# Four windowed-attention blocks on one core: constants loaded in two pieces, the first group's statistics gathered per image, bias tables on GpSimd, last stores in smaller parts

## The reference, cut to what matters

```
def _layernorm_hwc(x, scale, bias):                    # first block
    mean = jnp.mean(x, axis=(1, 2, 3), keepdims=True)
    var = jnp.var(x, axis=(1, 2, 3), keepdims=True)
    return (x - mean) * jax.lax.rsqrt(var + EPS) * scale + bias

attn = einsum('bhnd,bhmd->bhnm', q, k) + bias + mask    # blocks 2 to 4: one bias table, masks fixed by the window
x = x + softmax(attn) @ v @ proj_w + proj_b
m = gelu(_ln(x) @ fc1_w + fc1_b)                        # last block
x = x + _ln(m) @ fc2_w + fc2_b
```

## Time and profile before

| What | us |
|---|---|
| median of 3 runs | 7809.69 |
| lowest and highest of them | 7807.17, 7815.15 |
| the profiled execution's own time | 7816.85 |
| its span, first to last instruction | 7815.1 |

### The profile page before, as it was taken

One profiled execution on the slowest core, in us unless ns is written; L12 is line 12 of the kernel. 1 busy time (PEld: TensorE's weight loads), 2 busy tenths in 40 slices (PEclk: granted clock), 3 DMA queues, 4 the chain that ended last, 5 costly groups with the idle time before them and its releaser, 6 DMA issues.

```text
span 7815.1 us, 310674 instructions
## 1 busy us (share of the span) xinstructions
PE 7327.9 (94%) x109686; PEld 5700.3 (73%) x109686; DVE 6100.8 (78%) x18297; ACT 4899.6 (63%) x8745; POOL 5299.8 (68%) x6555
## 2 busy tenths in 40 slices
PE   5999999999899999999989999999999999999998
PEld 3777777777677777777767777777776777777777
DVE  6878878777786887877878687786787778778677
ACT  3746647557674765746767475574677647567467
POOL 4956657567795765757789476674778857567576
PEclk9999999999999999999999999999999999999999
DMA  2101101010110110101011011010101101011010
GB/s 62 39 11 30 52 12 33 11 36 17 25 40 30 35 47 17 33 7 43 10 31 51 19 34 43 22 33 7 45 4 37 57 11 33 14 27 30 11 42 25
DMA packets 309909, 227.60 MB, mean 29 GB/s; under 512 B 217379, under 2 KB 305766, under 8 KB 306344
## 3 DMA queue, kind: packets, MB, share of 16 engines
q1 hardware_dynamic: 307858, 215.98, 10.3%
q10 hardware_dynamic: 1622, 6.13, 0.2%
HBM read 117.62 MB, written 104.37 MB: 28 GB/s over the span
## 4 chain that ended last, share of the span: by engine, by line
POOL 35%; issue 27%; PE 22%; DVE 7%; POOLq 4%; DVEq 2%; ACT 1%; ACTq 0%
POOL S L654 17%; PE ps L1082 8%; PE ps L1055 7%; POOL G L644 7%; POOL xn L670 4%; POOL rstd L626 4%; DVE xn L1257 2%; DVE bst L1108 2%; PE ps L1069 2%; DVE x L1419 1%; PE ps L901 1%; DVEq L1257 1%; POOL mv L697 1%; PE ps L932 1%; POOLq L476 1%
## 5 line engine op out<-in xcount | busy, mean ns | idle before, releaser
L654 POOL TENSOR_TENSOR S<-S,mx 113x588 f32<-113x588 f32 (+1 forms) x2048 | 2059.0, 1009 | 896.3 <-DVE mx L1299 878.2
L777 ACT ACTIVATE S<-S 113x588 f32<-113x588 f32 (+1 forms) x2048 | 1246.9, 609 | 823.9 <-POOL S L654 809.2
L959 PE MATMUL ps<-turn,S 113*123 113x113 f32 (+2 forms) x8704 | 1329.2, 278 | 103.7 <-ACT PT L782 73.7
L1299 DVE TENSOR_REDUCE mx<-S 113x12 f32<-113x588 f32 (+1 forms) x2048 | 1359.4, 664 | 70.6
L782 ACT ACTIVATE PT<-ps 123x490 f32<-123x490 f32 (+1 forms) x2048 | 1051.1, 513 | 458.7 <-PE ps L959 438.6
L959 PEld LDWEIGHTS ps<-turn,S 113*123 113x123 f32 (+2 forms) x8704 | 927.7, 167 | 514.9 <-ACT PT L782 328.9
L1055 PEld LDWEIGHTS ps<-w,G 128*98 128x98 f32 x12288 | 1150.5, 167 | 159.3 <-issue 87.6
L1055 PE MATMUL ps<-w,G 128*98 128x96 f32 (+1 forms) x12288 | 1151.3, 250 | 0.0
L1082 PE MATMUL ps<-h,w 97*128 97x392 f32 x3072 | 1124.1, 502 | 9.1 <-ACT G L865 9.1
L1296 DVE TENSOR_TENSOR S<-ps,bias 113x588 f32<-113x588 f32 (+1 forms) x1536 | 963.9, 628 | 181.9 <-PE ps L948 135.2
L932 PEld LDWEIGHTS ps<-Va,PT 123*49 123x49 f32 (+1 forms) x18432 | 755.8, 125 | 326.3 <-ACT PT L782 255.0
(11 more groups left out here) (94 smaller groups left out, 12145.3 us busy)
## 6 DMA issues: line engine op xcount, KB each, us to landing
v_between<-Vd SPq DMA_DIRECT2D x384, 165.4 KB
Va<-v_between SPq DMA_DIRECT2D x768, 41.3 KB
Vb<-v_between SPq DMA_DIRECT2D x768, 27.6 KB
v_between<-Vd SPq DMA_DIRECT2D x128, 153.1 KB
Vl<-v_between SPq DMA_DIRECT2D x256, 76.6 KB
out_dram<-x SPq DMA_DIRECT2D x15, 1176.0 KB
x<-x_dram SPq DMA_DIRECT2D x14, 1176.0 KB
mask<-mask_dram SPq DMA_DIRECT2D x258, 37.5 KB
```

The source lines that it names most:

```text
L654: pool.tensor_tensor(v, v, m, ALU.subtract).then_inc(a_sub, 1)
L777: act.activation(S[:, p, 0:nh * N], S[:, p, 0:nh * N], ACT.Exp).then_inc(a_exp, 1)
L959: last = pe.transpose(ps[0:rows, PT_BANK, PAIR * b:PAIR * b + TOK], S[:, p, at:at + rows], turn[:, :])
L1299: dve.reduce_max(mx[:, s, 0:nh], S[:, s, 0:n].rearrange("p (h k) -> p h k", k=N), axis=AX.X).then_inc(a_mx, 1)
```

## The change

Four things are done. `load` splits a constant of 97 or 113 rows into its first 96 or 112 rows and its last row, two transfers. The 12 bias tables are made on POOL, ahead of its `fill`, as soon as the raw bias and `mask4` have landed, both counted on `s_braw`. The first group's statistics are taken as 32 `bn_stats` and one `bn_aggr` over all of them per image, which gives mean and variance of the image's pairs per partition at once; `norm` works on 4 columns in place of 128, has two `busy` matmuls fewer ahead of its second average, and takes up the correction of `w3` and `c2` while POOL raises to -0.5, so that PE waits for it only behind `norm`. At the end image 2 is stored when 24 quads are done, the first half of image 3 when 28 are, and its second half, in two parts from SP and ACT, behind `s_fin`.

```diff
+        def last_pairs(eng, a, b):
+            eng.dma_start(out[GROUPS - 1, :, a * C:b * C],
+                          x[:, (GROUPS - 1) % 2 * NP + a:(GROUPS - 1) % 2 * NP + b, :].rearrange("p a c -> p (a c)")
+                          ).then_inc(s_out, 16)
...
         def load(eng, dst, src):
-            eng.dma_start(dst, src).then_inc(s_const, 16)
-            n_const[0] += 16
+            rows = dst.shape[0]
+            cuts = (0, rows - 1, rows) if rows in (C + 1, TOK) else (0, rows)
+            for a, b in zip(cuts, cuts[1:]):
+                eng.dma_start(dst[a:b, :], src[a:b, :]).then_inc(s_const, 16)
+                n_const[0] += 16
...
             tokens(sp, GROUPS - 1, True, s_out, 0, IMGS // 2)
+            sp.wait_ge(m_res, GROUPS * LAYER_QUADS - NQ // 4)
+            tokens(sp, GROUPS - 1, True, s_out, IMGS // 2, IMGS - 1)
+            sp.wait_ge(m_res, GROUPS * LAYER_QUADS - NQ // 8)
+            last_pairs(sp, NP - 2 * 4 * QUAD, NP - 4 * QUAD)
             sp.wait_ge(s_fin, GROUPS)
-            tokens(sp, GROUPS - 1, True, s_out, IMGS // 2, IMGS, turn=0, turns=2)
+            last_pairs(sp, NP - 4 * QUAD, NP - 2 * QUAD)
...
             pool.wait_ge(s_memset, 2)
+            pool.wait_ge(s_braw, 32)
+            for l in range(1, LAYERS):
+                nh = HEADS[l]
+                for v in range(4):
+                    last = pool.tensor_tensor(bias[l][:, v, :].rearrange("p (h k) -> p h k", k=N),
+                                              stage(l).rearrange("p (h k) -> p h k", k=N),
+                                              mask4[:, v, :].unsqueeze(1).to_broadcast([P, nh, N]), ALU.add)
+            last.then_inc(s_tab, 1)
+            pool.wait_ge(s_tab, 1)
...
             act.wait_ge(s_fin, GROUPS)
-            tokens(act, GROUPS - 1, True, s_out, IMGS // 2, IMGS, turn=1, turns=2)
+            last_pairs(act, NP - 2 * QUAD, NP)
...
-            pe.wait_ge(s_w3, 2)
...
                     for n in range(2):
-                        busy(2, 4)
+                        busy(2, 4 if n == 0 else 2)
                         average_of(0, 0, 2, n)
+                    pe.wait_ge(s_w3, 2)
...
-            quad_steps(dve, 0, load_stats, 2, 0, NQ // 2)
-            dve.wait_ge(s_x, 16 * HALF_DMAS)
-            quad_steps(dve, 0, load_stats, 2, NQ // 2, NQ)
+            for image in range(IMGS):
+                if image == IMGS // 2:
+                    dve.wait_ge(s_x, 16 * HALF_DMAS)
+                for a in range(PAIRS_IMG):
+                    last = dve.bn_stats(bfirst[:, image, a, :], x[:, image * PAIRS_IMG + a, :])
+                last.then_inc(s_first, 1)
+                dve.wait_ge(s_first, image + 1)
+                dve.bn_aggr(ifirst[:, image, :], bfirst[:, image, :, :].rearrange("p a s -> p (a s)")).then_inc(s_gather, 1)
...
-            dve.wait_ge(s_w3ps, 1)
-            dve.tensor_tensor(w3[:, :, 0:C], w3[:, :, 0:C], ps[:, 0, 0:C].unsqueeze(1).to_broadcast([P, HC, C]),
-                              ALU.subtract)
-            dve.tensor_tensor(c2[:, LAYERS - 1, :], c2[:, LAYERS - 1, :], ps[:, 1, 0:C], ALU.add).then_inc(s_w3, 1)
...
...
                 def norm():
-                    image_sums(0, 0, 2)
-                    image_squares(0, 0, 2)
-                    image_var(0, 0, 2)
-                    image_scale(0, 0, 2)
+                    dve.tensor_scalar(isum[:, :], mean, float(PAIRS_IMG), None, ALU.mult).then_inc(s_avg, 1)
+                    dve.wait_ge(s_avg, 2)
+                    dve.tensor_copy(imean[:, :], ps[0:PAIR, O_BANK, 0:IMGS]).then_inc(s_chain, 1)
+                    dve.tensor_tensor(mean, mean, imean[:, :], ALU.subtract).then_inc(s_chain, 1)
+                    dve.tensor_tensor(mean, mean, mean, ALU.mult).then_inc(s_chain, 1)
+                    dve.tensor_tensor(mean, mean, var, ALU.add).then_inc(s_chain, 1)
+                    dve.tensor_scalar(isum[:, :], mean, float(PAIRS_IMG), None, ALU.mult).then_inc(s_avg, 1)
+                    dve.tensor_scalar(ivar[:, :], ps[0:PAIR, O_BANK, 0:IMGS], EPS, None, ALU.add).then_inc(s_nm, 1)
+                    dve.wait_ge(s_w3ps, 1)
+                    dve.tensor_tensor(w3[:, :, 0:C], w3[:, :, 0:C],
+                                      ps[:, 0, 0:C].unsqueeze(1).to_broadcast([P, HC, C]), ALU.subtract)
...
+                    dve.wait_ge(s_pow, 1)
+                    dve.tensor_copy(scales, irstd[:, :].unsqueeze(2).to_broadcast(every)).then_inc(s_chain, 1)
+                    dve.scalar_tensor_tensor(mean, imean[:, :], -1.0, irstd[:, :], ALU.mult,
+                                             ALU.mult).then_inc(s_chain, 1)
+                    dve.tensor_copy(shifts, mean.unsqueeze(2).to_broadcast(every)).then_inc(s_nmr, 1)
+                    dve.wait_ge(s_tab, 1)
```

More of the change, by code:

```diff
@@ L195, in build @@
         irstd = sb("irstd", [PAIR, IMGS])
+        ifirst = sb("ifirst", [PAIR, IMGS, 2])
         ident = sb("ident", [P, P])
@@ L240, in build @@
         shift3 = room[:, SHIFTS:SHIFTS + HC * P].rearrange("p (c q) -> p c q", c=HC)
+        bfirst = room[0:PAIR, SHIFTS + (HC + 1) * P:SHIFTS + (HC + 1) * P + 6 * NP].rearrange(
+            "p (i a s) -> p i a s", i=IMGS, s=6)
         share3 = room[:, SHIFTS + HC * P:SHIFTS + (HC + 1) * P]
@@ L289, in build @@
         s_w3 = sem("ln3_weights_scaled")
+        s_first = sem("first_image_stats")
+        s_gather = sem("first_image_gathered")
         s_w3ps = sem("ln3_weight_sums_done")
@@ L582, in _ @@
             tokens(sp, GROUPS - 1, True, s_out, 0, IMGS // 2)
+            sp.wait_ge(m_res, GROUPS * LAYER_QUADS - NQ // 4)
+            stand(sp)
+            tokens(sp, GROUPS - 1, True, s_out, IMGS // 2, IMGS - 1)
+            sp.wait_ge(m_res, GROUPS * LAYER_QUADS - NQ // 8)
+            stand(sp)
+            last_pairs(sp, NP - 2 * 4 * QUAD, NP - 4 * QUAD)
             sp.wait_ge(s_fin, GROUPS)
-            tokens(sp, GROUPS - 1, True, s_out, IMGS // 2, IMGS, turn=0, turns=2)
-            sp.wait_ge(s_out, (GROUPS - 1) * (16 * TOK_DMAS) + 2 * 16 * HALF_DMAS)
+            last_pairs(sp, NP - 4 * QUAD, NP - 2 * QUAD)
+            sp.wait_ge(s_out, (GROUPS - 1) * (16 * TOK_DMAS) + 16 * (IMGS - 1 + 3))
             stand(sp)
@@ L754, in _ @@
             load(act, bias[0][:, 0, :], d["bias0"])
-            load(act, mask4[:, :, :].rearrange("p a b -> p (a b)"), d["mask4"])
+            act.dma_start(mask4[:, :, :].rearrange("p a b -> p (a b)"), d["mask4"]).then_inc(s_braw, 16)
             act.dma_start(room[:, 0:STAGED], d["bias"]).then_inc(s_braw, 16)
@@ L1127, in all_stats @@
                 keep(u, at, n, t, ag, kept)
[L1131 to L1136, removed]
             dve.memset(mask0[:], 0.0).then_inc(s_maskpad, 1)
@@ L1143, in _ @@
             dve.wait_ge(s_x0, 16 * HALF_DMAS)
-            quad_steps(dve, 0, load_stats, 2, 0, NQ // 2)
-            dve.wait_ge(s_x, 16 * HALF_DMAS)
-            quad_steps(dve, 0, load_stats, 2, NQ // 2, NQ)
+            for image in range(IMGS):
[6 more added lines that the diff above has]
+                dve.bn_aggr(ifirst[:, image, :], bfirst[:, image, :, :].rearrange("p a s -> p (a s)")).then_inc(s_gather, 1)
+            dve.wait_ge(s_gather, IMGS)
+            for s in (x_bn, x_agg, x_mv):
+                dve.sem_inc(s, NQ)
             dve.wait_ge(s_const, n_const[0])
@@ L1244, in norm @@
                 def norm():
-                    image_sums(0, 0, 2)
-                    image_squares(0, 0, 2)
-                    image_var(0, 0, 2)
-                    image_scale(0, 0, 2)
+                    mean, var = ifirst[:, :, 0], ifirst[:, :, 1]
+                    every = [PAIR, IMGS, PAIRS_IMG]
+                    scales, shifts = (t[:, :].rearrange("p (i a) -> p i a", i=IMGS) for t in (vpe, nmr))
+                    dve.tensor_scalar(isum[:, :], mean, float(PAIRS_IMG), None, ALU.mult).then_inc(s_avg, 1)
+                    dve.wait_ge(s_avg, 2)
+                    dve.tensor_copy(imean[:, :], ps[0:PAIR, O_BANK, 0:IMGS]).then_inc(s_chain, 1)
+                    dve.wait_ge(s_chain, 1)
+                    dve.tensor_tensor(mean, mean, imean[:, :], ALU.subtract).then_inc(s_chain, 1)
+                    dve.wait_ge(s_chain, 2)
+                    dve.tensor_tensor(mean, mean, mean, ALU.mult).then_inc(s_chain, 1)
+                    dve.wait_ge(s_chain, 3)
+                    dve.tensor_tensor(mean, mean, var, ALU.add).then_inc(s_chain, 1)
+                    dve.wait_ge(s_chain, 4)
+                    dve.tensor_scalar(isum[:, :], mean, float(PAIRS_IMG), None, ALU.mult).then_inc(s_avg, 1)
+                    dve.wait_ge(s_avg, 4)
+                    dve.tensor_scalar(ivar[:, :], ps[0:PAIR, O_BANK, 0:IMGS], EPS, None, ALU.add).then_inc(s_nm, 1)
+                    dve.wait_ge(s_w3ps, 1)
+                    dve.tensor_tensor(w3[:, :, 0:C], w3[:, :, 0:C],
+                                      ps[:, 0, 0:C].unsqueeze(1).to_broadcast([P, HC, C]), ALU.subtract)
```

(9 more changed lines are left out.)

## The result

| What | before | changed |
|---|---|---|
| median, first comparison (5 runs each) | 7809.92 us | 7770.90 us |
| ratio, 95% interval | | 0.9945, 0.9933 to 0.9956 |
| median, second comparison (7 and 4 runs) | 7815.45 us | 7761.36 us |
| ratio, 95% interval | | 0.9937, 0.9920 to 0.9953 |
| span of the profiled execution | 7815.1 us | 7767.2 us |

The change takes 39 us off in one comparison and 54 in the other; 44.0 were forecast. In the profiled execution it is 47.9.

The account below looks back on a forecast made before the run. The prologue was taken as bound by constants on one DMA engine, then DVE's statistics, and the end by store bytes; 38.0 + 6.0 = 44.0 us less gave 7765.7 us, range 7752 to 7778.

Parts of the forecast that it names:

- One engine held the constants; a load of 96 rows spreads: Prologue loads: 97- or 113-row transfers use one DMA engine, 96 rows sit on 16; rival that constants stay late, 0.05.
- The constants' rate: Prologue: about 3.2 MB of constants left after the images move at 286 GB/s, raw bias landing at 31.5 us.
- A bias later than 34 us: Sign in the prologue: the raw bias landing after 34 us would mean the prediction is wrong.
- Statistics: DVE in the prologue: 128 bn_stats of 0.16 us, four aggregates, 2.2 us in all with waits; done at 35.7 us.
- POOL's additions: Prologue: twelve bias-table additions on POOL take 12.5 us, from 31.5 to 44.1 us; on DVE they cost nothing before.
- DVE waits until the burst ends: Prologue: DVE's three weight scalings at L1153 wait through all POOL table additions, done at 44.7 us.
- The second form of that rival: DVE gets past POOL, each scaling waiting for one 1.3 us addition: shift 56.2, time 7761.7; 0.27 for both forms.
- From the weights to the shift: Prologue from L1153 done to the shift done: 15.5 us in place of 18.1.
- The last step's 0.4 us: The step ending the shift becomes a short one and a copy: 0.4 us less, between 0.8 less and 2.8 more.
- The shift: End of the prologue, the moment that starts the pipeline: at 60.2 us in place of 98.2, 38.0 us less.
- The end: Last stores: 1.81 MB fewer left behind `s_fin`, 6.0 us less, 5 to 6.4.
- The middle is carried over: First shift to last quad stays 7705.1 us; a difference over 5 us would mean the prediction is wrong.

Follow-up runs that it names:

- `split_alone`: The kernel before with only the constants of 97 and 113 rows loaded as an even part and one row; 7796.48 us, ratio 0.9979.
- `early_bias`: The changed kernel with mask4 and the raw bias issued on ACT right behind the images, ahead of its other constants; 7759.89 us, ratio 0.9933 to the kernel before.
- `tail_alone`: The kernel before with only the last group's stores in smaller, earlier parts as in the change; 7804.43 us, ratio 0.9987.
- `two_inputs`: The changed kernel with the three weight scalings written as TENSOR_TENSOR with two inputs in SBUF; 7770.27 us, one run.
- `all_but_split`: The changed kernel with each constant loaded whole, as before; 7801.10 us, ratio 0.9988 to the kernel before.
- `pow_between`: The changed kernel with a short power of 98x4 ahead of each of POOL's twelve table additions; 7768.93 us, one run.
- `changed_again`: The changed kernel run once more, unchanged, against the kernel before; 7761.36 us beside 7815.45.

## Why the prediction was right, step by step

The time was right, and so was the mechanism of the loads, the statistics and the stores. How DVE fares beside POOL's burst was wrong, several sizes were off, and that these made up for each other is luck.

- *One engine held the constants; a load of 96 rows spreads.* Right: no issue of a constant lasts 20 us any more, and `split_alone` moves the first weight step to the end of the statistics. One issue still lasts longer than the few us that were forecast, `mask4`'s 10.61 us. *The constants' rate* was mis-sized: the raw bias let POOL start at 36.44 us, where 31.5 was forecast and 33.5 was the bound. The images took 2 us longer, and in the windows from 20 to 30 us the engines moved 223 and 191 GB/s and not 286. The long issue of `mask4` held the bias's own issue back to 18.62; in `early_bias`, with `mask4` in front, the two issues of `wp` that come at this time take 10.54 us, so it is not `mask4` itself. A bias later than 34 us was named as a sign that the prediction is wrong, and it cost something: PE waits for DVE's steps, and these for the burst's additions, so that in `early_bias` a burst 7.2 us earlier brought PE's start 4.9 us forward.
- *Statistics*: 0.16 us for each `bn_stats`, right. The aggregate was mis-sized, 1.02 us each in place of 0.3 to 0.5, and the first two images landed at 14.26 us, not 13.0. DVE was done at 38.86 in place of 35.7. In every kernel here with the split loads the images land at 13.7 to 14.7, in those without at 12.2 to 13.0.
- *POOL's additions*: 12.39 us, 12.5 forecast. Right. That the tables cost nothing on DVE before was wrong: DVE's first sums of `norm` stood behind them, and PE, through with its eight `busy` instructions, idled 0.86 us for these sums, in `tail_alone` 2.25 us. The row is of the kernel before, from PE's timeline.

```profile
91.08 0.34 PE L907 MATMUL ps<-isum,average 98*98 98x4 f32 x2 [0.86 <-DVE isum L1199]
```

- *DVE waits until the burst ends*: wrong. The second form of that rival, one wait of 1.3 us for each instruction, is what the rows show, in this kernel, in `two_inputs` and in `all_but_split`. It is what the Trainium skill's page SBUF — State Buffer, section "Who interferes with whom", has: the port pair is kept for a whole instruction. The prologue's rows beside additions agree (1.25 to 1.36 us a wait); the powers of `pow_between` and the end of the group loop don't. The weights were no sooner than forecast for it, because the copies ahead of L1153 wait as well (six waits, not three), DVE came 3.1 us later, and the burst began 4.9 us later. They were ready at 46.81, 44.7 forecast. Why a DVE addition waits 4.4 us at the end of the group loop, in the changed kernel again 4.34 us, and one addition only in the prologue, stays open. Such a wait comes once in each group of every run here, and always in the second half of a power with three additions right behind it; in the changed kernel the addition just ahead, which came earlier in the same power, passed:

```profile
7753.65 1.01 POOL L762 TENSOR_TENSOR r<-vp,neghalf 98x4 f32<-98x4 f32 x1 [2.68 <-DVE vp L1454]
7753.89 0.19 DVE L1227 TENSOR_TENSOR vpe<-mv,imean 98x32 f32<-98x32 f32 x1
7754.22 4.34 DVE L1230 TENSOR_TENSOR vpe<-vpe 98x32 f32<-98x32 f32 x1
7754.63 3.89 POOL L673 TENSOR_TENSOR G<-bias,mask 113x588 f32<-113x588 f32 x3
```

Two inputs in SBUF are not the cause by themselves (`two_inputs`, `all_but_split`), nor is a power by itself, since no DVE instruction that came beside one in `pow_between` waited for the addition behind it. Both together, an addition with two inputs that comes late in a power, were not tried in the prologue.

- *From the weights to the shift*: 12.77 us in place of 15.5. The sum had the correction (0.7) and POOL's power right. What it had too long was the way to the first average, 4.89 us from the first `busy` instruction in place of 7.35: PE no longer idles 0.86 us for DVE's sums, and the first eight instructions took 5.05 us in place of 6.49, since they went from one every 0.86 us to one every 0.43 after the third step and not in the seventh. The last step's 0.4 us didn't come: its copy waited for one of POOL's mask additions and took 1.24 us. The quicker `busy` was not the change: `tail_alone`, with the prologue before, has 5.10 us for the eight in this row of its PE timeline.

```profile
82.78 5.10 PE L913 MATMUL ps<-w,ident 128*128 128x512 f32 x8 [0.71 <-DVE c L1170]
```

- *The shift*: 59.57 for 60.2, a gain of 38.6 for 38.0. +2.1 in the weights and -2.7 behind them cancelled, for reasons that have nothing to do with each other.
- *The end*: 6.1 us less from issue to end, 6.0 forecast. Right. The issue followed the last quad 0.35 us later than before (2.13 for 1.78), so 5.7 net.
- *The middle is carried over*: within the scatter. In the profiled execution it was 3.6 us shorter, which with 38.6 + 5.7 makes the 47.9 of the span. In `changed_again` it was 15.7 us shorter, where over 5 was to mean that the prediction is wrong; that sign was drawn too tight, as the three kernels with the old statistics differ by 6.5 us among themselves.

## What to carry to other kernels

A load of 97 or 113 rows can hold up all that is queued behind it: look for a long stretch at a sixteenth of the DMA share and for an issue that lasts tens of us, and take the odd row off. Parts that each remove one of two limits in a row must be costed together, since each alone shows only the distance to the other. Work that is moved to POOL is not off DVE's path merely because POOL is idle: see which DVE steps run beside it, and move the load that starts it, or leave it on DVE under a PE stretch that hides it, behind the sums that PE waits for.

## What the runs showed of the hardware that was not expected

- From 20 to 30 us, while the last of the images and the constants landed, DMA engines that were 94 to 95% busy moved 223 and 191 GB/s, fewer than the 286 of the stores at a share of 0.77. The runs don't show why.
- A `bn_aggr` took 1.02 us over 192 elements, 5.3 ns each, where a `bn_stats` took 0.16 us over 96, 1.7 ns each.
- A DVE copy or scaling of 0.22 to 0.26 us, and an addition of 0.16 us, each waited for a POOL addition of 1.3 us to end, one after the other; the POOL burst itself was not longer for it (12.39 us, and 12.38 in `early_bias`, where its long additions ran mostly beside DVE's statistics, which don't wait).
- The moment from which PE's `busy` matmuls run at double rate varies between the executions here: from one to six full steps of about 0.86 us come ahead of those of 0.43, three and six with the same prologue (`tail_alone` and the kernel before). The granted clock's column doesn't show it: in the changed kernel it reads 1.00 from 49.5 to 52 us and from 52 to 54.5.
